# A graph-network and feed-forward kernel: a weight sum moved from GpSimd to VectorE in the opening of the first batch, with the message bias behind it and two distance products some taps later

## Chip, cores and metric

The kernel runs on 1 core of one Trainium2 chip. The metric is the device time of one execution in microseconds. The kernel is written with explicit queues: each engine (TensorE, called PE in the profile; VectorE, DVE; ScalarE, ACT; GpSimd, POOL; SyncE, SP) works through its own list of instructions in order, and semaphores tie the lists together.

## The reference

The input is `x` of 8 batches x 1024 nodes x 128 features and an adjacency `adj` of 8 x 1024 x 1024. A layer norm feeds a graph layer, whose result is added to `x`; a second layer norm feeds a feed-forward layer of the 511 highest-weighted nodes of each batch. What matters here is the graph layer:

```python
xc = jnp.transpose(x, (0, 2, 1))
h = _bn(_conv1d(xc, conv1_w, 0), bn1_g, bn1_b, bn1_m, bn1_v)
h = jax.nn.relu(h)
h = _bn(_conv1d(h, conv2_w, 8), bn2_g, bn2_b, bn2_m, bn2_v)
x_conv = jnp.transpose(jax.nn.relu(h + xc), (0, 2, 1))
s = x @ w_se.T + b_se
sq = jnp.sum(s * s, axis=-1)
dist = sq[:, :, None] + sq[:, None, :] - 2.0 * jnp.einsum('bnd,bmd->bnm', s, s)
A = jnp.exp(-dist) * mask
msg = jax.nn.relu(x @ w_msg.T + b_msg)
x_nmp = jnp.einsum('bnm,bmd->bnd', A, msg)
```

`conv2_w` is 128 x 128 x 17, a convolution of 17 taps along the nodes; `mask` is `adj`. A GRU cell joins `x_conv`, `x_nmp` and `x`.

## The kernel before, in words

**Batches.** A loop over 8 batches runs on every engine; `step(b, ...)` is one batch, and the branches marked `first` are the opening, in which the weights are made ready too. Each batch has: transposition of the normed nodes, the convolution of one tap (`conv1`), the embedding `s`, the messages, the 17-tap convolution, 16 units of distances and adjacency (`adjacency`), and the GRU.

**Two-part numbers.** Products are made in three passes (`three`, L1381 to L1383): weights and data are split into a rounded part ("hi", made by a ScalarE copy) and the rest ("lo", made by a VectorE subtraction). `hi_of_weights(n)` and `lo_of_weights(n)` (L845 and L1016) do so for one piece of the weights, and count `wH_ok` and `wL_ok`.

**The 17-tap convolution** is cut by node parity and tap parity, and each part again, so that sums of taps stand in for some of the taps. PE works through it in five parts: `conv_common` (sums of all), `conv_even_common` (5 taps on `eF`, weights W_PE), `conv_even` (9 taps, weights W_WE), and `conv_odd` (12 taps numbered n = 0 to 11: n = 0 to 3 into bank N1 with weights W_PO, n = 4 to 11 into bank C0 with weights W_WO). Each tap is three matmuls of 128x256. The weights of W_PE and W_PO are sums of two halves of the raw even and odd taps, 128x512 each; `pairs_of_taps(0)` and `pairs_of_taps(1)` (L555) make them on GpSimd into `raw_p`, which lies in the tile `W`. The data of the convolution are differences of phases: `junk` holds `eF` and `fF` (L608, GpSimd), `EF2` (L598 and L599 into `xn`) and `EF3` (L598 and L599 into `tr`) are made on GpSimd, and each is split by ScalarE (L689, L699) and VectorE (L1041 odd row, L1045 pair) into `zR`. `zL_ok` counts these; its sixth step, ZEF3, is the pair of EF3.

**Distances.** `front(b, u)` is a distance product (L1519, one matmul of 128x512 from `U` and `V`) and four transposes of the adjacency (L1525). Three fronts are woven into `conv_odd`, by the table `EARLY`: ahead of taps n = 3, 7 and 11. Front 0 waits for two `distance_operands` on VectorE (L1095, one half of U, one of V), front 1 for the third. From front 3 on, a front is followed by one product with the messages (L1548), three units behind. Each unit on VectorE is one `weigh` (L1127).

**What stands in `conv_odd`'s way.** Ahead of n = 0 it waits for `lo_of_weights(W_PO)` and the odd row of fF; ahead of n = 4 for `common_of_b` (L1051) and for ZEF3:

```python
if row == 1:
    i.then_inc(cc_ps, 1)
    wait(pe, g1_ok, b, 1, 1)
    wait(pe, zL_ok, b, NZ, ZEF3)
for k in range(KQ):
    if n in EARLY:
        front(b, EARLY[n])
```

`add_msg_bias` (L1086) adds the message bias on VectorE, two halves that read PSUM banks D0 and D1; `relu_msg` on ScalarE follows it.

Of the kernel before, what the change touches and what calls it, by code (L numbers as in the profile page):

```python
# [19 lines left out]
ALU = mybir.AluOpType  # L20
# [6 lines left out]
D = 128  # L27
# [12 lines left out]
KQ = KO // 2  # L40
# [17 lines left out]
UV_FOR = {0: 2, 1: 3, NU // 2: 4}  # L58
N2_AT = (5, 6, 7, 8)
EARLY = {3: 0, 7: 1, 11: 2}  # L60


C_ID, C_TRI, C_MASK = 0, P, 2 * P
# [83 lines left out]
def build(nc, x, adj, vectors, weights, conv2_w, const, out):  # L147
    ctx = ExitStack()
    with ctx:
# [6 lines left out]
        def sem(name):  # L156
            return ctx.enter_context(nc.semaphore(name))
# [78 lines left out]
        raw_p = W  # L236
# [35 lines left out]
        stats1, rstd0_ok, rstd_ok, xn_ok = sem("stats1"), sem("rstd0_ok"), sem("rstd_ok"), sem("xn_ok")  # L272
        mom1, mom2, agg = sem("mom1"), sem("mom2"), sem("agg")
        xT_ps, xT_ok, xTH_ok, xTL_ok = sem("xT_ps"), sem("xT_ok"), sem("xTH_ok"), sem("xTL_ok")
        sum_w, pair_w = sem("sum_w"), sem("pair_w")
        c1_ps, ab_ok, z_ok, zH_ok, zL_ok = sem("c1_ps"), sem("ab_ok"), sem("z_ok"), sem("zH_ok"), sem("zL_ok")
        ef1_ok = sem("ef1_ok")
        p1_ps, c1s_ok, g1_ok, gs_ok = sem("p1_ps"), sem("c1s_ok"), sem("g1_ok"), sem("gs_ok")
# [81 lines left out]
        def taps(at, n):  # L360

            return slice(at * D, (at + n) * D)
# [12 lines left out]
        RAW_E, RAW_O = raw_t[:, taps(T_WE - T_S, KO)], raw_t[:, taps(T_WO - T_S, KO)]  # L375
# [110 lines left out]
        def _(pool):  # L486
# [53 lines left out]
            def inv_std2():  # L540
# [8 lines left out]
            nc.gpsimd.memset(blank[:, 0:R_AT], 0.0).then_inc(blank_ok, 1)  # L549
            nc.gpsimd.iota(blank[:, R_AT:R_AT + 1].bitcast(I32), [[1, 1]], base=B * N,  # L550
                           channel_multiplier=0).then_inc(blank_ok, 1)
            def pairs_of_taps(k):

                raw = (RAW_E, RAW_O)[k]
                nc.gpsimd.tensor_tensor(raw_p[:, k * KQ * D:(k + 1) * KQ * D], raw[:, 0:KQ * D], raw[:, KQ * D:],  # L555
                                        ALU.add).then_inc(pair_w, 1)

            def row_numbers(b, q):
# [71 lines left out]
            def step(b, q, first, last):  # L630
                differences(b, 0)
                if first:
                    pool.wait_ge(c2_in, 16)
                    wait(pool, zL_ok, b, NZ, ZEF1)
                    pairs_of_taps(0)
                differences_of_e(b)
                if not first:
                    state_less_candidate(b - 1, 1, 1 - q)
                differences(b, 1)
                if first:  # L640
                    pairs_of_taps(1)
                differences_of_f(b)
                residual(b, q, 0)
                residual(b, q, 1)
                if first:
                    statistics1(1)
                else:
                    statistics2(b - 1)
                    row_numbers(b - 1, 1 - q)
                    products(b - 1, 1 - q)  # L650
                    base_rows(b - 1, 1 - q)
                    if b > 1:
                        rows_by_rank(b - 2, q, 0)
                        rows_by_rank(b - 2, q, 1)
                if b + 2 < B:
                    statistics1(b + 2)
                state_less_candidate(b, 0, q)
# [16 lines left out]
        def _(act):  # L674
# [87 lines left out]
            def normalise2(b, q, ts):  # L762

                if ts[0] == 0:
                    wait(act, rstd2_ok, b, 1, 1)
                    wait(act, x1_ok, b, NH, NH)
                    if b == 0:
                        act.wait_ge(wL_ok, W_PO + 1)
                        act.wait_ge(pair_w, 2)
                    for s_, v in scattered(q, b):  # L770
                        if v > 0:
                            act.wait_ge(s_, v)
                for t in ts:
                    i = nc.scalar.activation(R[:, q, t, 0:D], xall[:, b % NX, t, :], ACT.Identity,
                                             bias=nmr2[:, b, t:t + 1], scale=rstd2[:, b, t:t + 1])
                if ts[-1] == T - 1:
                    i.then_inc(xn2_ok, 1)
# [75 lines left out]
            def step(b, q, first, last):  # L853
                relu_conv1(b)
                hi_of_odd(b, 0, hab[:, 1, :], ab_ok, NH, NH)
                if first:
                    act.wait_ge(sum_w, 2)
                    hi_of_weights(W_SC)
                    hi_of_weights(W_S)
                hi_of_pair(b, 0, EF1, 0)  # L860
                if first:
                    hi_of_odd(b, 1, eF, z_ok, E_AT, N_DIFF)
                    hi_of_weights(W_WO)
                    embed(b, q, 0)
                    common_part(b)
                    act.wait_ge(pair_w, 1)
                    hi_of_weights(W_PE)
                    embed(b, q, 1)
                    hi_of_pair(b, 1, EF2, EF2_AT)
                    embed_hi(b, q)  # L870
                else:
                    candidate(b - 1, 1)
                    embed(b, q, 0)
                    hi_of_odd(b, 1, eF, z_ok, E_AT, N_DIFF)
                    hi_of_pair(b, 1, EF2, EF2_AT)
                    embed(b, q, 1)
                    common_part(b)
                    embed_hi(b, q)
                hi_of_odd(b, 0, fF, z_ok, F_AT, N_DIFF)
                if first:  # L880
                    act.wait_ge(pair_w, 2)
                    hi_of_weights(W_PO)
                distance_hi(b, q, 0)
                hi_of_pair(b, 0, EF3, EF3_AT)
                distance_hi(b, q, 2)
                relu_msg(b)
                exps(b)
                if not last:
                    copy_xT(b + 1, 1 - q)
                hi_of_nmp(b)  # L890
                if first:
                    act.wait_ge(prep_dve, N_PARAM)
                gates(b, 0)
                candidate(b, 0)
                if last:
                    hi_of_sel(0, 0)
                gates(b, 1)

            over_batches(act, step)


# [36 lines left out]
        def _(dve):  # L938
            TS, TT, STT = nc.vector.tensor_scalar, nc.vector.tensor_tensor, nc.vector.scalar_tensor_tensor
# [73 lines left out]
            def lo_of_weights(n):  # L1013
                raw, dst = PIECES[n]
                dve.wait_ge(wH_ok, HI_ORDER.index(n) + 1)
                TT(dst[:, 1], raw, f32(dst[:, 0]), ALU.subtract).then_inc(wL_ok, 1)  # L1016
# [30 lines left out]
            def common_of_b(b):  # L1047

                wait(dve, p1_ps, b, 2, 2)
                wait(dve, c1s_ok, b, 1, 1)  # L1050
                STT(phases(G1), phases(C0[:, :]), col(V_SC2), on_phases(C1S), ALU.mult, ALU.add).then_inc(g1_ok, 1)  # L1051
# [29 lines left out]
            def add_msg_bias(b):  # L1081
                for h in range(NH):
                    wait(dve, m_ps, b, NH, h + 1)
                    if h == 0:
                        wait(dve, nm_ps, b - 1, NU, NU)
                    TT(msgF[:, h * TH:(h + 1) * TH, :], Db[h][:, :].rearrange("p (t d) -> p t d", t=TH),  # L1086
                       bmsg.unsqueeze(1).broadcast_to([P, TH, D]), ALU.add).then_inc(mb_ok, 1)
# [100 lines left out]
            def step(b, q, first, last):  # L1188
# [8 lines left out]
                if first:  # L1197
                    lo_of_weights(W_WE)
                    lo_of_odd(b, 1, eF, ZE)
                    lo_of_weights(W_PE)  # L1200
                    add_msg_bias(b)
                    lo_of_pair(b, 1, EF2, ZEF2)
                    lo_of_weights(W_WO)
                    lo_of_odd(b, 0, fF, ZF)
                    lo_of_weights(W_PO)
                    common_of_b(b)
                else:
                    add_msg_bias(b)
                    lo_of_odd(b, 1, eF, ZE)
                    lo_of_pair(b, 1, EF2, ZEF2)  # L1210
                    blend(b - 1, 1)
                    common_of_b(b)
                    lo_of_odd(b, 0, fF, ZF)
# [162 lines left out]
        def _(pe):  # L1376
# [78 lines left out]
            def conv_odd(b):  # L1455
                if b == 0:
                    pe.wait_ge(wL_ok, W_PO + 1)
                wait(pe, zL_ok, b, NZ, ZF)
                n = 0
                for out_, at, row in ((N1[:, 0:Q], T_WOC, 0), (C0[:, 0:Q], T_WO, 1), (C0[:, Q:2 * Q], T_WO + KQ, 2)):  # L1460
                    if row == 1:
                        i.then_inc(cc_ps, 1)
                        wait(pe, g1_ok, b, 1, 1)
                        wait(pe, zL_ok, b, NZ, ZEF3)
                    for k in range(KQ):
                        if n in EARLY:
                            front(b, EARLY[n])
                        n += 1
                        cols = slice(k, k + Q)
                        i = three(out_, lambda v: wc2[:, v, (at + k) * D:(at + k + 1) * D], zR[:, 0, 0, row, cols],  # L1470
                                  zR[:, 1, 0, row, cols], k == 0, k == KQ - 1)
                i.then_inc(c2_ps, 1)
# [233 lines left out]
```

## Time and profile before

| what | value |
|---|---|
| median of 3 runs | 562.78 us (562.45 to 562.78) |
| the profiled execution | 561.96 us, of which 560.1 us lie between its first and last instruction |
| PE busy | 544.9 us, 97% of the span |
| DVE busy | 475.0 us, 85% |
| ACT busy | 355.2 us, 63% |
| POOL busy | 276.1 us, 49% |

The opening of the first batch, from 10 to 37 us, is where the change lies. Times in the rows are microseconds from the start of the span, unless marked ns. A row of the timeline gives the start, the time taken, the engine, the source line, the operation, output<-inputs, and, in brackets, how long the engine was idle before it and what ended the idling. Consecutive instructions of one engine overlap by some 0.1 us in such rows, so the step from one start to the next is what an instruction costs in a row of them.

### The profile page before, as it was taken

What the parts mean: (1) busy time and instruction counts of PE and PEld (TensorE: products, weight loads), DVE (VectorE), ACT (ScalarE), POOL (GpSimd) and SP (SyncE); (2) the same over time, 40 slices, a digit from 0 to 9 for tenths busy, and PEclk for the clock granted to TensorE, in tenths of its full rate; (3) what the DMA queues carried; (4) which work ended last, traced back from release to release, by engine and by line L of the source; (5) the groups of instructions that cost most, each with busy time, mean ns of one, the idle gap of its engine ahead of it and who ended that gap; (6) DMA issues with size and microseconds to landing.
All of it is one profiled execution on the core that took longest, in us unless ns stands there. A gap on an engine that the chain in (4) does not pass through costs nothing.

```text
span 560.1 us, 9036 instructions
## 1 busy us (share of the span) xinstructions
PE 544.9 (97%) x2964; PEld 414.8 (74%) x2964; DVE 475.0 (85%) x1056; ACT 355.2 (63%) x617; POOL 276.1 (49%) x346
## 2 busy tenths in 40 slices
PE   7899999999999999999999999999999999989996
PEld 4876798678967896689767986798678966755663
DVE  7997388689898989899999989898979987988722
ACT  5867485856586667748674857575856673645552
POOL 3640354325358444834484546654545265437552
PEclk9999999999999999999999999999999999999999
DMA  8703700270008200750057001800171005402102
GB/s 276 280 0 80 297 0 2 71 305 1 2 11 294 109 2 1 208 207 1 1 136 278 1 2 54 323 2 1 46 282 49 1 1 180 160 12 85 38 33 62
DMA packets 33340, 54.53 MB, mean 97 GB/s; under 512 B 2098, under 2 KB 23051, under 8 KB 33166
## 3 DMA queue, kind: packets, MB, share of 16 engines
q1 hardware_dynamic: 29710, 48.42, 24.8%
q0 software_dynamic: 3584, 5.54, 2.9%
q8 instruction: 24, 0.39, 0.3%
q14 instruction: 22, 0.18, 0.1%
HBM read 44.21 MB, written 13.43 MB: 103 GB/s over the span
## 4 chain that ended last, share of the span: by engine, by line
PE 81%; DVE 11%; issue 3%; ACT 3%; POOL 1%; DMA 0%; DVEq 0%; ACTq 0%; POOLq 0%
PE N L1548 19%; PE M L1525 10%; PE C L1381 7%; PE C L1382 6%; PE C L1383 6%; PE D L1519 5%; PE N L1642 4%; PE N L1381 3%; PE N L1382 3%; PE N L1383 3%; ACT hab L681 2%; PE M L1382 2%; PE M L1381 2%; PE M L1383 2%; DVE tr L1036 2%
## 5 line engine op out<-in xcount | busy, mean ns | idle before, releaser
L787 ACT ACTIVATE tr<-D 128x512 f32<-128x512 f32 x128 | 76.4, 597 | 75.6 <-PE D L1519 73.9
L1525 PEld LDWEIGHTS M<-cst,adjb 128*128 128x128 f32 x512 | 63.8, 141 | 35.5 <-issue 20.8
L1519 PE MATMUL D<-V,U 128*128 128x512 f32 x128 | 89.3, 698 | 0.7 <-DVE V L1095 0.7
L1525 PE MATMUL M<-cst,adjb 128*128 128x128 f32 x512 | 76.8, 272 | 0.6 <-DVE ga L1127 0.6
L581 POOL DMA_INDIRECT sel<-R,ridx x56 | 61.1, 1090 | 16.0 <-issue 13.8
L1548 PE MATMUL N<-ga,msgF 128*128 128x512 f32 x128 | 64.2, 593 | 0.0
L1548 PE MATMUL N<-tz,msgF 128*128 128x512 f32 x128 | 64.2, 593 | 0.0
L1381 PE MATMUL C<-zR,wc 128*128 128x256 f32 x208 | 60.6, 291 | 0.1
L1382 PE MATMUL C<-zR,wc 128*128 128x256 f32 x208 | 58.6, 282 | 0.0
L1383 PE MATMUL C<-zR,wc 128*128 128x256 f32 x208 | 58.5, 281 | 0.0
L1157 DVE TENSOR_SCALAR_CACHE_REDUCE junk<-W,R 128x1024 bf16<-128x1024 f32 (+3 forms) x64 | 51.7, 808 | 3.7 <-ACT W L749 3.7
L1127 DVE TENSOR_TENSOR ga<-tr,M 128x512 f32<-128x512 f32 x64 | 43.5, 680 | 9.5 <-ACT tr L787 9.3
L1127 DVE TENSOR_TENSOR tz<-tr,M 128x512 f32<-128x512 f32 x64 | 43.7, 684 | 7.9 <-ACT tr L787 6.1
L528 POOL TENSOR_TENSOR ga<-xT,gn 128x512 f32<-128x512 f32 x16 | 22.8, 1423 | 43.7 <-ACT gn L839 42.8
L1519 PEld LDWEIGHTS D<-V,U 128*128 128x128 f32 x128 | 24.3, 190 | 23.8 <-ACT tr L787 19.1
L1151 DVE TENSOR_SCALAR_CACHE_REDUCE junk<-W,R 128x128 bf16<-128x128 f32 (+6 forms) x56 | 41.4, 739 | 0.0
L627 POOL TENSOR_TENSOR wk<-tz,xT 128x512 f32<-128x512 f32 x8 | 12.5, 1558 | 58.0 <-DVE tz L1058 58.0
L608 POOL TENSOR_TENSOR junk<-hab 128x521 f32<-128x521 f32 x16 | 19.6, 1225 | 40.8 <-ACT hab L681 40.8
L1381 PEld LDWEIGHTS C<-zR,wc 128*128 128x128 f32 x208 | 39.2, 189 | 0.3 <-issue 0.3
L1383 PEld LDWEIGHTS C<-zR,wc 128*128 128x128 f32 x208 | 39.4, 189 | 0.0
L1382 PEld LDWEIGHTS C<-zR,wc 128*128 128x128 f32 x208 | 39.3, 189 | 0.0
L592 POOL DMA_INDIRECT out<-xn,adjb x28 | 28.4, 1015 | 18.7 <-DVE xn L1311 12.3
(245 smaller groups left out, 1523.9 us busy)
## 6 DMA issues: line engine op xcount, KB each, us to landing
adjb<-in_adj SPq DMA_DIRECT2D x8, 4096.0 KB, 14.9
adjb<-sel SPq DMA_DIRECT2D x7, 516.0 KB, 5.3
xall<-in_x SPq DMA_DIRECT2D x7, 512.0 KB, 5.3
out<-R SPq DMA_DIRECT2D x7, 512.0 KB, 3.6
R<-in_conv_w SPq DMA_DIRECT2D x1, 1088.0 KB, 7.1
sel<-R,ridx POOLq DMA_INDIRECT x56, 3.5
xall<-in_weights SPq DMA_DIRECT2D x1, 832.0 KB, 9.8
xall<-in_x SPq DMA_DIRECT2D x2, 256.0 KB, 2.8
```

The lines of the kernel that those rows point to most:

```text
L581: nc.gpsimd.indirect_dma_start(sel[b], bass.IndirectOffsetOnAxis(ap=ridx[:, q, t:t + 1], axis=0), R[:, q, t, :], None, bounds_check=KEEP - ...
L592: nc.gpsimd.indirect_dma_start(out_rows, bass.IndirectOffsetOnAxis(ap=at, axis=0), O[:, p, c, :], None, bounds_check=B * N - 1, oob_is_err ...
L787: nc.scalar.activation(E[:, u % NE, :], Db[u % NH][:, :], ACT.Exp, scale=-1.0).then_inc(exp_ok, 1)
L1127: TT(A[u % NA], E[:, u % NE, :], Mb[u % NH][:, :], ALU.mult).then_inc(A_ok, 1)
L1151: TS(junk[:, t % 2, 0:t * P], W[:, 0:t * P], R[:, q, t, R_W:R_W + 1], None, ALU.is_ge, ALU.add, accum_out=acc[:, 0, t:t + 1])
L1157: TS(junk[:, k, t * P:N], W[:, t * P:], w, None, ALU.is_gt, ALU.add, accum_out=acc[:, 1, t:t + 1])
L1381: MM(out_, wgt(0), hi, start=start, stop=False)
L1382: MM(out_, wgt(0), lo, start=False, stop=False)
L1383: return MM(out_, wgt(1), hi, start=False, stop=stop)
L1519: MM(Db[h][:, :], U[:, t * P:(t + 1) * P], V[:, half(h)], start=True, stop=True).then_inc(d_ps, 1)
L1525: i = TR(Mb[h][:, k * P:(k + 1) * P], adjb[:, h * TH + k, t * P:(t + 1) * P], ident)
L1548: MM(Nb[h][:, :], msgF[:, t, :], A[v % NA], start=t == 0, stop=t == T - 1).then_inc(nm_ps, 1)
```

## The change

Three edits, all of which touch the first batch alone:

1. `pairs_of_taps(1)`, the sum for W_PO, is no longer on GpSimd. VectorE makes it right behind `lo_of_weights(W_PE)`, and a semaphore of its own, `pair_o`, tells ScalarE.
2. `add_msg_bias` moves on VectorE from behind `lo_of_weights(W_PE)` to behind `lo_of_weights(W_PO)`.
3. In the first batch fronts 0 and 1 stand ahead of taps n = 7 and n = 9 and no longer of n = 3 and n = 7; front 2 stays at n = 11.

```diff
+EARLY_0 = {7: 0, 9: 1, 11: 2}
...
                 differences(b, 1)
-                if first:
-                    pairs_of_taps(1)
                 differences_of_f(b)
...
                 if first:
-                    act.wait_ge(pair_w, 2)
+                    act.wait_ge(pair_o, 1)
                     hi_of_weights(W_PO)
...
                     lo_of_weights(W_PE)
-                    add_msg_bias(b)
+                    TT(raw_p[:, KQ * D:], RAW_O[:, 0:KQ * D], RAW_O[:, KQ * D:], ALU.add).then_inc(pair_o, 1)
                     lo_of_pair(b, 1, EF2, ZEF2)
                     lo_of_weights(W_WO)
                     lo_of_odd(b, 0, fF, ZF)
                     lo_of_weights(W_PO)
+                    add_msg_bias(b)
                     common_of_b(b)
...
                     for k in range(KQ):
-                        if n in EARLY:
-                            front(b, EARLY[n])
+                        early = EARLY_0 if b == 0 else EARLY
+                        if n in early:
+                            front(b, early[n])
```

VectorE's list in the opening, from `lo_of_weights(W_PE)` to `common_of_b`, before:

```order
L1016 TENSOR_TENSOR wc<-W,wc 128x512
L1086 TENSOR_TENSOR msgF<-D,vec 128x512 x2
L1045 TENSOR_TENSOR zR<-xn,zR 128x520
L1016 TENSOR_TENSOR wc<-R,wc 128x1024
L1041 TENSOR_TENSOR zR<-junk,zR 128x260
L1016 TENSOR_TENSOR wc<-W,wc 128x512
L1051 SCALAR_TENSOR_TENSOR tz<-C,vec,tr 128x512
```

and of the changed kernel (its line numbers are lower by one up to the new line 1200):

```order
L1015 TENSOR_TENSOR wc<-W,wc 128x512
L1200 TENSOR_TENSOR W<-R 128x512
L1044 TENSOR_TENSOR zR<-xn,zR 128x520
L1015 TENSOR_TENSOR wc<-R,wc 128x1024
L1040 TENSOR_TENSOR zR<-junk,zR 128x260
L1015 TENSOR_TENSOR wc<-W,wc 128x512
L1085 TENSOR_TENSOR msgF<-D,vec 128x512 x2
L1050 SCALAR_TENSOR_TENSOR tz<-C,vec,tr 128x512
```

The pair sum `W<-R` stands where the two halves of the message bias stood, and these are now the last work ahead of `common_of_b`. Behind it both lists go on alike.

GpSimd's list over the same stretch, before:

```order
L555 TENSOR_TENSOR W<-R 128x512
L598 TENSOR_TENSOR xn<-junk 128x260
L599 TENSOR_TENSOR xn<-junk 128x260
L608 TENSOR_TENSOR junk<-hab 128x521
L555 TENSOR_TENSOR W<-R 128x512
L598 TENSOR_TENSOR tr<-junk 128x260
L599 TENSOR_TENSOR tr<-junk 128x260
L627 TENSOR_TENSOR wk<-tz,xT 128x512
```

The second `L555` is gone in the changed kernel, and the rest stands in the same order.

PE's list in `conv_odd`, from the last matmul of tap n = 3 over the taps n = 4, 5 and 6 to front 0 ahead of n = 7, in the changed kernel:

```order
L1383 MATMUL N<-zR,wc 128x256
L1381 MATMUL C<-zR,wc 128x256
L1382 MATMUL C<-zR,wc 128x256
L1383 MATMUL C<-zR,wc 128x256
L1381 MATMUL C<-zR,wc 128x256
L1382 MATMUL C<-zR,wc 128x256
L1383 MATMUL C<-zR,wc 128x256
L1381 MATMUL C<-zR,wc 128x256
L1382 MATMUL C<-zR,wc 128x256
L1383 MATMUL C<-zR,wc 128x256
L1520 MATMUL D<-V,U 128x512
L1526 MATMUL M<-cst,adjb 128x128 x4
```

Before, a `L1519` and its `L1525 x4` stood three matmuls ahead of the first of these C rows, between the taps n = 2 and n = 3. Now nothing but convolution stands ahead of n = 4's wait for EF3.

## Rows read from the trace of the kernel before

**Rows 1.** The page: busy time of each engine, share of the span, instructions

```profile
PE 544.9 (97%) x2964; PEld 414.8 (74%) x2964; DVE 475.0 (85%) x1056; ACT 355.2 (63%) x617; POOL 276.1 (49%) x346
```

**Rows 2.** Waits of PE from 10 to 75 us: total us, times, longest

```profile
PE N L1381 <- DVE wc L1016: 1.3, 2, 0.9
```

**Rows 3.** Timeline of PE in the opening

```profile
23.93 0.36 PE L1381 MATMUL C<-zR,wc 128*128 128x256 f32 x1
...
27.12 0.28 PE L1383 MATMUL C<-zR,wc 128*128 128x256 f32 x1
27.87 0.38 PE L1381 MATMUL N<-zR,wc 128*128 128x256 f32 x1 [0.47 <-DVE wc L1016]
...
29.94 0.47 PE L1519 MATMUL D<-V,U 128*128 128x512 f32 x1 [0.74 <-DVE V L1095]
...
30.60 0.36 PE L1381 MATMUL N<-zR,wc 128*128 128x256 f32 x1
...
31.03 0.28 PE L1381 MATMUL C<-zR,wc 128*128 128x256 f32 x1
...
35.24 0.40 PE L1519 MATMUL D<-V,U 128*128 128x512 f32 x1
```

**Rows 4.** Timeline of DVE in the opening

```profile
12.91 0.69 DVE L1187 TENSOR_TENSOR R<-R 128x512 f32<-128x512 f32 x1
...
20.99 0.69 DVE L1016 TENSOR_TENSOR wc<-W,wc 128x512 fp32r<-128x512 f32 x1 [0.41 <-ACT wc L845]
21.60 1.28 DVE L1086 TENSOR_TENSOR msgF<-D,vec 128x512 f32<-128x512 f32 x2
22.94 0.85 DVE L1045 TENSOR_TENSOR zR<-xn,zR 128x520 fp32r<-128x520 f32 x1
23.71 2.31 DVE L1016 TENSOR_TENSOR wc<-R,wc 128x1024 fp32r<-128x1024 f32 x1
25.94 0.84 DVE L1041 TENSOR_TENSOR zR<-junk,zR 128x260 fp32r<-128x260 f32 x1
26.71 1.10 DVE L1016 TENSOR_TENSOR wc<-W,wc 128x512 fp32r<-128x512 f32 x1
27.74 0.74 DVE L1051 SCALAR_TENSOR_TENSOR tz<-C,vec,tr 128x512 f32<-128x512 f32 x1
...
29.72 0.69 DVE L1045 TENSOR_TENSOR zR<-tr,zR 128x520 fp32r<-128x520 f32 x1
...
36.41 0.67 DVE L1127 TENSOR_TENSOR ga<-tr,M 128x512 f32<-128x512 f32 x1
```

**Rows 5.** Timeline of POOL in the opening

```profile
13.31 1.25 POOL L608 TENSOR_TENSOR junk<-hab 128x521 f32<-128x521 f32 x1 [3.86 <-ACT hab L681]
...
21.02 1.14 POOL L599 TENSOR_TENSOR xn<-junk 128x260 f32<-128x260 f32 x1
22.12 1.11 POOL L608 TENSOR_TENSOR junk<-hab 128x521 f32<-128x521 f32 x1
23.20 1.74 POOL L555 TENSOR_TENSOR W<-R 128x512 f32<-128x512 f32 x1
24.89 1.61 POOL L598 TENSOR_TENSOR tr<-junk 128x260 f32<-128x260 f32 x1
26.46 0.80 POOL L599 TENSOR_TENSOR tr<-junk 128x260 f32<-128x260 f32 x1
```

**Rows 6.** Timeline of ACT: the hi parts of EF2 and of fF

```profile
22.27 0.64 ACT L699 ACTIVATE zR<-xn 128x520 fp32r<-128x520 f32 x1
...
23.85 0.43 ACT L689 ACTIVATE zR<-junk 128x260 fp32r<-128x260 f32 x1
```

**Rows 7.** The chain that ended last, just behind the opening: start, us, what

```profile
37.17 0.61 PE M L1525 x4
```

**Rows 8.** Windows at the span's end: busy time, granted clock, DMA

```profile
557.00:558.00 1.00, 0.00 (x0) 0.00 (x0) 0.27 (x2) 0.00 (x0) 0.00 (x0) 1.00 0.00 0
558.00:559.00 1.00, 0.00 (x0) 0.00 (x0) 0.00 (x0) 0.00 (x0) 0.00 (x0) 1.00 0.75 220
559.00:560.10 1.10, 0.00 (x0) 0.00 (x0) 0.00 (x0) 0.00 (x0) 0.00 (x0) 0.66 0.14 38
```

More of the change, by code:

```diff
@@ L274, in build @@
         xT_ps, xT_ok, xTH_ok, xTL_ok = sem("xT_ps"), sem("xT_ok"), sem("xTH_ok"), sem("xTL_ok")
-        sum_w, pair_w = sem("sum_w"), sem("pair_w")
+        sum_w, pair_w, pair_o = sem("sum_w"), sem("pair_w"), sem("pair_o")
         c1_ps, ab_ok, z_ok, zH_ok, zL_ok = sem("c1_ps"), sem("ab_ok"), sem("z_ok"), sem("zH_ok"), sem("zL_ok")
@@ L551, in _, with pairs_of_even_taps @@
                            channel_multiplier=0).then_inc(blank_ok, 1)
-            def pairs_of_taps(k):
-                raw = (RAW_E, RAW_O)[k]
-                nc.gpsimd.tensor_tensor(raw_p[:, k * KQ * D:(k + 1) * KQ * D], raw[:, 0:KQ * D], raw[:, KQ * D:],
+            def pairs_of_even_taps():
+                nc.gpsimd.tensor_tensor(raw_p[:, 0:KQ * D], RAW_E[:, 0:KQ * D], RAW_E[:, KQ * D:],
                                         ALU.add).then_inc(pair_w, 1)
@@ L634, in step @@
                     wait(pool, zL_ok, b, NZ, ZEF1)
-                    pairs_of_taps(0)
+                    pairs_of_even_taps()
                 differences_of_e(b)
@@ L768, in normalise2 @@
                         act.wait_ge(wL_ok, W_PO + 1)
-                        act.wait_ge(pair_w, 2)
+                        act.wait_ge(pair_w, 1)
+                        act.wait_ge(pair_o, 1)
                     for s_, v in scattered(q, b):
@@ L880, in step @@
                 if first:
-                    act.wait_ge(pair_w, 2)
+                    act.wait_ge(pair_o, 1)
                     hi_of_weights(W_PO)
```

## The prediction

> **What bounds the kernel now.** I read the page first: PE is busy for 97% of the span [rows 1], so a microsecond counts only where PE loses it, and what PE loses early is lost at the end, unless a later wait takes it up. Next I asked for PE's waits from 10 to 75 us. In the stretch of the change, from 21 us on, they are two: 0.47 us ahead of `conv_odd`'s first tap, for `lo_of_weights(W_PO)`, and 0.74 us ahead of front 0, for the second distance operand [rows 2, 3]. (The 1.3 us of rows 2 hold the first of these and one wait near 16 us, ahead of all that is changed.) Behind front 0 the list of waits names no other, so nothing up to 75 us can take up a delay. The third view was the timeline of DVE and POOL side by side. The reader is to see there that DVE works without a pause from 20.99 us to the distances, so that it sets when W_PO, the operands and EF3 are ready, and that some of its rows are long for their size [rows 4].
>
> Those rows are the key. A subtraction of 128x512 takes 0.69 us at 20.99 and 1.10 us at 26.71; one of 128x260 takes 0.84 us at 25.94, longer than the 0.69 us of one twice its size. Each long row began while a POOL operation was under way, and ended a fixed time behind it [rows 4, 5]:
> - POOL L555 ends at 24.94, the DVE 128x1024 at 26.02: 1.10 us after it, about its bare time.
> - POOL L598 ends at 26.50, the DVE 128x260 at 26.78: 0.28 after it.
> - POOL L599 ends at 27.26, the DVE 128x512 at 27.81: 0.55 after it. For the 128x520, 23.23 to 23.79: 0.56.
>
> It holds the other way too. POOL's 128x260 takes 0.80 us by itself and 1.61 at 24.89; it ends 0.48 us behind the DVE operation that ends at 26.02, as the one at 26.46 ends 0.48 behind 26.78, and that at 21.02 ends 0.48 behind 21.68. L608 ends 0.96 behind the DVE end at 13.60 [rows 4, 5]. So an operation of DVE with both inputs in SBUF and one of POOL exclude each other and take turns. The message bias, which reads PSUM, takes 1.28 us for two beside a POOL operation: it does not take part.
>
> The Trainium skill (SBUF — State Buffer, "Who interferes with whom") states this as an exclusive hold for the whole instruction, between a VectorE instruction with two SBUF inputs and a GpSimd one that reads SBUF; the rows agree. It speaks against a hope in this change, that a POOL operation was free for DVE or is free now.
>
> **The change part by part.** I walk both lists from 20.99 us, where nothing has changed yet, with the turn-taking above. Ends in brackets are those of before.
> - `lo_of_weights(W_PE)` ends at 21.68 (21.68). POOL L599, which waits for it, ends at 22.16 (22.16).
> - New pair sum on DVE. No row shows it on this engine. It has the size of the 128x512 subtractions: 0.69 us bare, 0.55 behind a release, 1.10 if blocked [rows 4]; 0.55 to 1.10 bounds it. It comes at 21.60, is blocked until 22.16, and ends at 22.71. I take that.
> - POOL L608 (fF) was free here; now it ends 0.96 behind, at 23.67 (23.23).
> - EF2's pair on DVE: its hi part is there at 22.91 [rows 6], so it is behind L608: 23.67 + 0.56 = 24.23 (23.79).
> - POOL L598 comes next, as L555 with its 1.74 us is gone: 24.71. DVE 128x1024: + 1.10 = 25.81 (26.02). POOL L599: 26.29 (27.26). DVE odd row of fF: + 0.29 = 26.58 (26.78); its hi part, 0.43 us behind L608 [rows 6], is long done.
> - `lo_of_weights(W_PO)` starts at 26.50 with POOL idle: 0.69, so 27.19 (27.81). Its hi part needs the pair sum of 22.71, and ScalarE comes to it behind fF, near 24.3: no wait.
> - Message bias: two PSUM reads, start at 27.11, and the next instruction can start 1.22 us later, at 28.33. `common_of_b` started at 27.74 [rows 4].
>
> So DVE gives back 0.6 us of blocking and takes on 1.22 us: from `common_of_b` on, everything is 0.59 us later. EF3's pair started at 29.72 and ended at 30.41 [rows 4]; now it ends at 31.00. The moved bias itself costs nothing further: ScalarE's relu of the messages came behind its distance operands, near 29.3, and the bias ends at 28.4.
>
> PE now. `conv_even` waits for EF2's pair and started at 23.93, 0.14 behind it; now 24.37. Its 27 matmuls took 23.93 to 27.24, 3.31 us or 0.368 a tap [rows 3], so it ends at 27.68. W_PO is there (27.19), so the wait of 0.47 is gone: `conv_odd` starts at 27.7 (27.87), a gain of 0.2. Four taps take it to 29.15. There it stops, at n = 4, for EF3 until 31.1: a wait of 2 us in place of the 0.74. Before, front 0 and tap n = 3 stood across this moment, and EF3 (30.41) was ready when PE came to n = 4 at 31.03 [rows 3, 4]. The later place of fronts 0 and 1 takes away the one piece of work that could lie ahead of EF3. Had front 0 stayed at n = 3, its operands would be ready 0.59 later too, at 30.4, ahead of EF3.
>
> From n = 4 to front 3, eight taps and fronts 1 and 2 took 31.03 to 35.24, 4.21 us. Now front 0 is in the stretch as well, 0.66 us (29.94 to 30.60), and a tap behind a wait costs 0.1 more (0.38 against 0.28 in its first row) [rows 3]. So front 3 starts at 31.1 + 4.21 + 0.66 + 0.1 = 36.07, against 35.24: 0.83 later. A little comes back at once. The transposes of front 4 took 0.61 in the chain where the others take 0.44 [rows 7], since they waited 0.17 us for the third `weigh`, which ended at 37.08 [rows 4]; that is now 0.59 later, at 37.67, and PE comes there at 37.83, so the wait is gone: 0.83 - 0.17 = **0.66 us later**. Moving fronts 0 and 1 to 7 and 9 keeps their exponentials ahead of front 2, and `weigh` 0 at 33.8 and 1 at 34.8 ahead of fronts 2 and 3: no new wait.
>
> The sum is made in the profiled execution: 561.96 + 0.66 = 562.6 us. That execution is 0.82 below the median of the runs; against the median 562.78 the forecast is 563.4 us. What a measurement of this kernel can tell from no change is about 0.2%, or 1.1 us; so I forecast no measurable difference, on the slow side.
>
> **The rivals.**
> - *The lock gives nothing back (slower).* If POOL's phase differences take the port at worse moments, for instance just ahead of `lo_of_weights(W_PO)` so that it again takes 1.10 us and ends at 27.8, the full 1.22 of the bias plus the 0.14 for PE's restart falls on EF3 and PE: front 3 about 1.45 late, 1.3 at the end, 564.1. It decides the sign from 1.13 us on, that is when W_PO ends later than about 27.65. For it: before, the DVE operation was blocked at just this place. Against it: one POOL operation of four is gone. A milder form, in which DVE wins the first turn at 21.60, gives W_PO at 27.49, 0.3 later than forecast, and the end near 563.7. Chance 17%.
> - *No blocking of the new order (faster, too little to measure).* If DVE were never blocked, EF2's pair would end at 23.6, 0.15 earlier, with 24.8 for the 128x1024 and about 25.7 for W_PO; PE's `conv_even` would end near 27.1 and EF3's pair near 29.5, so PE waits 1 us and front 3 starts at 34.45, 0.8 early: 562.0. Against it stand all the long rows. Chance 12%.
> - *The clock falls in the new 2 us wait.* Then the stretch behind it, 4.97 us long, runs at 1.2 instead of 2.4 GHz and costs up to 5 us more: 568. Against it: at the span's end PE does nothing from 557 to 559, and the granted clock is still 1.00 in both windows, and falls only in the next [rows 8]. Chance 3%.
>
> The Trainium skill (TensorE: Matmul & The Clock Gate, "Part 1") makes the slow clock the default that activity lifts, and that a long idle stretch brings back; by that rule a wait of 2 us is a step toward it. The rows at the end show 2 us at least without it.
>
> That the change does nothing at all is excluded: the lists of all three engines differ as described.
>
> **How the numbers follow.** The forecast has 68%, with 562.9 to 563.9 as its own range (the 0.55 to 1.10 of the pair sum, either winner of the turns, 0.3 us of spread between runs). To leave out no more than 2 in 10 the range takes in the slower rival and leaves out the fast one and the clock: 562.3 to 564.4. Faster by over 0.2% (under 561.65) needs more than the fast rival: 0.04. Slower by over 0.2% (over 563.91): most of the slower rival, the clock, a tail of the forecast: 0.20. Same: 0.76.
>
> **What would show it.** In the changed profile: PE idle 0 ahead of `conv_odd`'s first tap, and about 2 us ahead of the first C tap, ended by DVE's zR from `tr`; the pair sum on DVE 1.1 us long, started at 21.6; W_PO's subtraction 0.69 long, ended near 27.2; `common_of_b` at 28.3; front 3 at 36.1; transposes of front 4 at 37.8. The prediction is wrong if the wait ahead of n = 4 is under 1.2 us, if the DVE rows stay long where POOL is idle, or if PE finds another wait behind 37 us in which 0.66 us vanish.

## The result and the profile after

| | before | changed |
|---|---|---|
| median, 20 runs each | 562.78 us (562.15 to 563.5) | 563.34 us (562.7 to 565.03) |
| ratio | | 1.0013, 95% interval 1.0007 to 1.0019 |
| profiled execution | 561.96 us, span 560.1 | 564.65 us, span 562.6 |

The changed kernel is 0.13% slower, 0.4 to 1.1 us: a loss too small for the 0.2% of a single comparison, and visible with 20 runs on each side. The forecast was 563.4. But its executions spread over 2.3 us where those of before spread over 1.4, and the profiled one is the second slowest of the 20, so its trace has to be read in two parts.

The first part is the opening itself. The rows of DVE in the changed kernel, by the timeline:

```profile
21.48 0.69 DVE L1015 TENSOR_TENSOR wc<-W,wc 128x512 fp32r<-128x512 f32 x1 [0.41 <-ACT wc L844]
22.09 1.10 DVE L1200 TENSOR_TENSOR W<-R 128x512 f32<-128x512 f32 x1
23.42 1.30 DVE L1044 TENSOR_TENSOR zR<-xn,zR 128x520 fp32r<-128x520 f32 x1 [0.23 <-ACT zR L697]
24.64 1.64 DVE L1015 TENSOR_TENSOR wc<-R,wc 128x1024 fp32r<-128x1024 f32 x1
26.20 0.84 DVE L1040 TENSOR_TENSOR zR<-junk,zR 128x260 fp32r<-128x260 f32 x1
26.97 0.68 DVE L1015 TENSOR_TENSOR wc<-W,wc 128x512 fp32r<-128x512 f32 x1
27.57 1.27 DVE L1085 TENSOR_TENSOR msgF<-D,vec 128x512 f32<-128x512 f32 x2
28.77 0.73 DVE L1050 SCALAR_TENSOR_TENSOR tz<-C,vec,tr 128x512 f32<-128x512 f32 x1
...
30.75 0.69 DVE L1044 TENSOR_TENSOR zR<-tr,zR 128x520 fp32r<-128x520 f32 x1
```

and those of POOL beside them:

```profile
22.61 1.55 POOL L608 TENSOR_TENSOR junk<-hab 128x521 f32<-128x521 f32 x1
24.24 0.96 POOL L598 TENSOR_TENSOR tr<-junk 128x260 f32<-128x260 f32 x1
25.16 1.60 POOL L599 TENSOR_TENSOR tr<-junk 128x260 f32<-128x260 f32 x1
```

In this execution W_PE's subtraction starts at 21.48 where it started at 20.99 [rows 4], so all that comes before the change was 0.49 us late, and 0.49 is to be taken off every time of this trace. Then the reader sees the walk of the prediction: the pair sum blocked to 1.10 us and ended at 22.70 (forecast 22.71), EF2's pair at 24.23 (24.23), W_PO at 27.16 (27.19), `common_of_b` started at 28.28 (28.33), EF3 ended at 30.95 (31.00). W_PO's subtraction is 0.68 us long, with POOL idle, where it was 1.10 [rows 4].

The rows of PE in the changed kernel:

```profile
24.86 0.36 PE L1381 MATMUL C<-zR,wc 128*128 128x256 f32 x1 [0.58 <-DVE zR L1044]
...
28.15 0.28 PE L1381 MATMUL N<-zR,wc 128*128 128x256 f32 x1
...
31.58 0.36 PE L1381 MATMUL C<-zR,wc 128*128 128x256 f32 x1 [1.84 <-DVE zR L1044]
...
38.12 0.39 PE L1520 MATMUL D<-V,U 128*128 128x512 f32 x1
```

The wait ahead of `conv_odd`'s first tap is gone and 1.84 us stand ahead of n = 4, ended by EF3's pair, as forecast. The last row is front 3. Less 0.49, it starts at 37.63, and the forecast was 36.07: 1.56 us too many.

The second part is where these went. Windows of the changed kernel: length, busy time of PE, PE's weight loads, DVE, ACT and POOL, granted clock, DMA share, GB/s:

```profile
28.00:32.00 4.00, 2.16 (x18) 1.99 (x17) 4.00 (x7) 1.89 (x4) 0.00 (x0) 1.00 0.00 0
32.00:36.00 4.00, 4.00 (x22) 3.65 (x21) 2.77 (x5) 0.75 (x2) 2.43 (x2) 0.61 0.00 0
36.00:40.00 4.00, 4.00 (x28) 3.28 (x27) 3.37 (x11) 1.64 (x3) 1.53 (x6) 0.97 0.00 0
```

and the chain that ended last, in that stretch (start, length, what):

```profile
32.77 0.12 PE C L1383
32.89 0.36 PE D L1520
33.25 0.85 PE M L1526 x4
34.11 0.21 PE C L1381
...
35.39 0.43 PE D L1520
35.81 0.72 PE M L1526 x4
36.53 0.12 PE C L1381
```

The granted clock is 0.61 in the mean from 32 to 36 us: TensorE went from 2.4 to 1.2 GHz, and not in the wait but 1.3 us after its end. Through the wait itself the clock reads 1.00 (28 to 32 us). The matmul of a tap takes 0.21 us in place of 0.12, a distance product 0.36 to 0.43 in place of 0.24, and four transposes 0.72 to 0.85 in place of 0.44. From 32.89 to 36.53 these pieces add up to 3.64 us; at the durations around them they would be 2.08. The difference, 1.56, is the whole of the surplus.

Of the 20 executions of the changed kernel 4 show a mean clock of 0.996 and spans of 562.2 to 562.6 us, while the other 16 have 0.997 or more and 560.9 to 561.9. The span is the time from the first to the last instruction. By this the fall comes in some executions only and costs 1.45 us by the medians of the spans, and the median of all 20 hardly holds it. Not every high time is a fall: two executions of 564.12 and 564.18 us have spans of 561.2 and 561.3, so what they lost lies outside the span.

### The profile page after: what moved, and what is told of

It is laid out like the page before. It is cut to its first block, busy times and chain, and to the rows that moved or that the text cites. A ratio compares the mean times of both kernels' runs of the same rounds, so it can differ in the third digit from the quotient of the medians.

```text
span 562.6 us, 9036 instructions
## 1 busy us (share of the span) xinstructions
PE 545.6 (97%) x2964; PEld 415.9 (74%) x2964; DVE 475.6 (85%) x1057; ACT 355.0 (63%) x617; POOL 274.5 (49%) x345
## 4 chain that ended last, share of the span: by engine, by line
PE 82%; DVE 9%; ACT 3%; issue 3%; POOL 1%; DMA 1%; DVEq 0%; ACTq 0%; POOLq 0%
PE N L1549 20%; PE M L1526 10%; PE C L1381 7%; PE C L1382 6%; PE C L1383 6%; PE D L1520 5%; PE N L1643 4%; PE N L1381 3%; PE N L1382 3%; PE N L1383 3%; ACT hab L679 2%; PE M L1382 2%; PE M L1381 2%; PE M L1383 2%; DVE tr L1035 2%
```

## The experiments

Every ratio is against runs of the kernel before on the same chip, with its 95% interval. To compare profiles, whose openings start up to half a microsecond apart, I also give times from the start of the first sum of the raw taps (DVE, `R<-R 128x1024`, 11.66 us in before). On that scale front 3 starts at 23.58 us in before, W_PO ends at 16.15, and the second batch's transposes start at 44.51.

### e1. Edit 3 alone: the fronts late

```diff
+EARLY_0 = {7: 0, 9: 1, 11: 2}
...
-                        if n in EARLY:
-                            front(b, EARLY[n])
+                        early = EARLY_0 if b == 0 else EARLY
+                        if n in early:
+                            front(b, early[n])
```

> Edit 3 alone: fronts 0 and 1 late, the pair sum and the message bias as before. Turn-taking theory: VectorE and GpSimd keep every start of before, EF3's pair ends at 30.4, PE comes to tap n = 4 near 29.4 and waits 1.1 to 1.2 us there; front 3 starts 0.28 us later than before (in a profile whose VectorE list runs at the same times), and 0.17 comes back at front 4: +0.1 us, ratio 1.0002. Clock theory (a wait of PE of about 2 us lets TensorE's clock fall in part of the executions): this wait is the shorter one, granted clock 1.00 and no execution over 563.9. Rival (the late fronts themselves cost, by exponentials and weigh steps that come late): +0.5 us or more with the clock at 1.00.

Measured: 562.91 us, ratio 0.9997 (0.9988 to 1.0006), highest execution 563.43. PE's rows:

```profile
30.75 0.36 PE L1382 MATMUL C<-zR,wc 128*128 128x256 f32 x1 [0.98 <-DVE zR L1046]
...
35.69 0.40 PE L1521 MATMUL D<-V,U 128*128 128x512 f32 x1
```

The wait stands at n = 4, 0.98 us (forecast 1.1 to 1.2), and front 3 starts at 23.82, 0.24 later (forecast 0.28). The second batch's transposes start at 44.58, 0.07 later. Edit 3 costs nothing that can be measured, and its rival is out.

### e2. The change without edit 3

```diff
-                        early = EARLY_0 if b == 0 else EARLY
-                        if n in early:
-                            front(b, early[n])
+                        if n in EARLY:
+                            front(b, EARLY[n])
```

> The change without edit 3: pair sum on VectorE, bias late, fronts at n = 3, 7 and 11. Turn-taking theory: VectorE's list is that of the changed kernel, front 0 waits for the second operand until about 0.6 us later than before, and the third weigh, 0.59 late, sets front 4: +0.6 us, ratio 1.0010. Clock theory: PE's wait is about 1.5 us in place of 1.84, the clock may still fall in some executions; if it does not, the highest execution stays below 564.3. Rival (edit 3 is what costs): back to 562.8.

Measured: 563.6 us, ratio 1.0010 (1.0001 to 1.0019), highest 563.8; PE waits 1.60 us ahead of front 0, and no execution shows the clock below 0.998. So the loss belongs to edits 1 and 2, and the late fronts neither caused it nor gave anything back that could be measured. With front 0 at n = 3 the wait is 0.24 us shorter, and no execution shows a fallen clock. That the shorter wait is the reason is not shown: if 4 in 20 executions fell here as well, 11 in a row without a fall would still come about one time in twelve, and e4 shows falls with front 0 at n = 3.

### e3. Edit 1 alone: the pair sum on VectorE

GpSimd's second sum goes, VectorE makes it, the bias comes directly behind it, and the fronts are those of before.

```diff
                     lo_of_weights(W_PE)
+                    TT(raw_p[:, KQ * D:], RAW_O[:, 0:KQ * D], RAW_O[:, KQ * D:], ALU.add).then_inc(pair_o, 1)
                     add_msg_bias(b)
```

> Edit 1 alone: the pair sum on VectorE, the message bias directly behind it (it was directly behind W_PE), fronts as before. Turn-taking theory: W_PO's subtraction ends near 27.5 in place of 27.8, common_of_b and all behind it start 0.3 us earlier, PE waits as before for operands, front 3 0.3 us earlier: -0.3 us, ratio 0.9995. Rival (an added VectorE operation costs its 0.6 us, since VectorE is the engine that PE waits for): +0.6 us, ratio 1.001.

Measured: 562.82 us, ratio 0.9994 (0.9985 to 1.0003). DVE's rows:

```profile
22.01 1.10 DVE L1200 TENSOR_TENSOR W<-R 128x512 f32<-128x512 f32 x1
...
24.24 1.10 DVE L1044 TENSOR_TENSOR zR<-xn,zR 128x520 fp32r<-128x520 f32 x1
25.26 1.64 DVE L1015 TENSOR_TENSOR wc<-R,wc 128x1024 fp32r<-128x1024 f32 x1
26.82 0.41 DVE L1040 TENSOR_TENSOR zR<-junk,zR 128x260 fp32r<-128x260 f32 x1
27.16 0.68 DVE L1015 TENSOR_TENSOR wc<-W,wc 128x512 fp32r<-128x512 f32 x1
```

VectorE got one operation more, blocked to 1.10 us, and `common_of_b` starts 0.38 us earlier (15.70 against 16.08), as do front 3 (23.21, 0.37 earlier) and the second batch (44.13). PE's wait is not where it was forecast. It stands ahead of `conv_even`, for EF2's pair, which is 1.15 us later behind the pair sum and the bias, and PE no longer stops for W_PO and only 0.1 us for front 0:

```profile
25.48 0.36 PE L1381 MATMUL C<-zR,wc 128*128 128x256 f32 x1 [1.27 <-DVE zR L1044]
```

The rival, that an operation added to the engine that is waited for costs its length, would have been +0.6. Taking an operation off GpSimd gave VectorE more than the operation cost it. The interval of the times holds 1; the trace shows the sign.

### e4. Edit 2 alone: the bias late

```diff
-                    add_msg_bias(b)
                     lo_of_pair(b, 1, EF2, ZEF2)
...
                     lo_of_weights(W_PO)
+                    add_msg_bias(b)
```

> Edit 2 alone: the message bias behind W_PO, the pair sum on GpSimd, fronts as before. Turn-taking theory: VectorE stands idle 1.2 us ahead of EF2's pair, nothing is blocked less, all from common_of_b on is 1.22 us later, and so is front 0: +1.2 us with the clock up, ratio 1.0022. Clock theory: PE waits about 2.1 us for the second operand, as long as in the changed kernel or longer; the clock falls in at least a part of the executions and adds about 1.5 us to those: spread to 565.5. Rival (the bias is hidden wherever it stands): within 0.3 us of before.

Measured: 564.24 us, ratio 1.0026 (1.0017 to 1.0035). Three of 11 executions show a clock of 0.995 and spans of 563.3 to 563.6, the other eight spans of 562.0 to 562.6. The bias late costs 1.2 us by itself (median span 562.3 against 561.1 of before on this chip), and the clock sometimes another 1.3. Both theories hold so far. The pause of DVE in this kernel:

```profile
21.63 1.00 DVE L1016 TENSOR_TENSOR wc<-W,wc 128x512 fp32r<-128x512 f32 x1 [1.86 <-ACT wc L845]
23.57 1.84 DVE L1045 TENSOR_TENSOR zR<-xn,zR 128x520 fp32r<-128x520 f32 x1 [0.94 <-ACT zR L699]
```

It stands idle for 0.94 us where the bias was, and makes the bias up at the end. `common_of_b` starts 1.44 us later than before, 0.2 more than forecast, and the first row shows where 0.2 can come from: W_PE's subtraction ended 0.68 later than in before (see e9). PE waits 1.56 us ahead of front 0 in this trace, and the clock stays up. The three executions that fell have no trace. If W_PE was on time in them, the wait was near 2.0 us (an estimate: the 0.74 of before and the bias's 1.22), so it is not known to be 1.56.

### e5. PE's wait filled

```diff
                     if row == 1:
+                        if b == 0:
+                            for _ in range(14):
+                                i = MM(N1[:, Q:2 * Q], wc2[:, 0, T_WOC * D:(T_WOC + 1) * D], zR[:, 0, 0, 0, 0:Q],
+                                       start=True, stop=True)
                         i.then_inc(cc_ps, 1)
```

> The changed kernel with 14 extra matmuls of 128x256 on PE between tap n = 3 and the wait ahead of n = 4, into a part of bank N1 that nobody reads: 14 x 0.118 = 1.65 us of work in a wait of 1.84. Nothing is left out. Turn-taking theory alone: the wait shrinks to 0.2 us, PE goes on at the same time, the time is that of the changed kernel with all its spread. Clock theory: the clock stays at 1.00 from 24 to 44 us, no execution over 563.9, median 563.2 to 563.4. Rival (the executions above 564 of the changed kernel have another cause): the highest executions stay at 564.5 to 565.

Measured: 563.63 us (563.33 to 563.82), ratio 1.0012 (1.0003 to 1.0021), span 561.5 to 561.9 in all 11. From 28 to 32 us, and from 32 to 36, in the columns of the windows above:

```profile
28.00:32.00 4.00, 4.00 (x36) 4.00 (x35) 4.00 (x7) 2.01 (x4) 0.00 (x0) 1.00 0.00 0
32.00:36.00 4.00, 4.00 (x34) 3.76 (x33) 3.51 (x6) 1.20 (x2) 2.21 (x2) 1.00 0.00 0
```

The high executions are gone, and what stays by the times is 0.66 us (563.63 against 562.97), the size of the forecast. In the trace W_PE's subtraction ended late (10.70), and the second batch starts at 45.39, 0.88 later than before. With that lateness PE's wait ahead of n = 4 would have been about 1.4 us without the filling (an estimate: against e0 below, PE is 0.68 later and EF3 0.27), and the 14 matmuls cover it with 0.2 to spare.

### e0. The changed kernel again, on the same chip

> The changed kernel once more, beside the filled one on the same chip: ratio 1.0010 to 1.0016, between a tenth and four tenths of its executions 0.8 us or more above the rest. Clock theory: a profile of it shows the clock at 1.00 or fallen for some 3 us behind 32 us, as the execution falls.

Measured: 564.98 us (563.43 to 565.37), ratio 1.0032 (1.0020 to 1.0043). Four of seven executions have a clock of 0.995 or 0.996 and spans of 563.2 to 563.3; the other three have 0.998 or more and 561.6 to 562.2. More than the one to four tenths that I expected fell. The profile is of one that did not:

```profile
28.00:32.00 4.00, 2.16 (x19) 1.99 (x18) 4.00 (x8) 1.74 (x3) 0.00 (x0) 1.00 0.00 0
32.00:36.00 4.00, 4.00 (x35) 3.77 (x33) 3.50 (x7) 1.41 (x3) 2.58 (x2) 1.00 0.00 0
```

and its wait ahead of n = 4:

```profile
31.43 0.36 PE L1381 MATMUL C<-zR,wc 128*128 128x256 f32 x1 [1.84 <-DVE zR L1044]
```

Its wait is 1.84 us as well and PE is busy for 2.16 us between 28 and 32, but 35 matmul records stand from 32 to 36 us, not 22. On the common scale every row of VectorE from W_PE to EF3 and the end of PE's wait agree with the trace that fell, to 0.02 us. Front 3 starts at 24.37, 0.79 later than before (forecast 0.83), and the second batch 0.61 later (forecast 0.66). Beside the filled kernel, on the same chip, this shows the cause of the large spread: with the stretch 4 of 7 executions fell, with the stretch filled 0 of 11. The three with the clock up have a median of 563.66 us, 0.69 above before; the four others lie 1.4 above these (spans 563.25 against 561.9), and between the two traces the second batch differs by 1.6 (46.73 and 45.12).

### e6. EF3's pair ahead of the operands

```diff
+                if first:
+                    lo_of_pair(b, 0, EF3, ZEF3)
                 distance_operands(b, q, (0, 1))
-                lo_of_pair(b, 0, EF3, ZEF3)
+                if not first:
+                    lo_of_pair(b, 0, EF3, ZEF3)
```

> The changed kernel with EF3's subtraction ahead of the first two distance operands on VectorE. Turn-taking theory: EF3 ends 1.3 us earlier, the wait ahead of n = 4 falls from 1.84 to about 0.6 us, front 3 starts 1.2 us earlier than in the changed kernel; but the third weigh, which comes behind moments1 on VectorE, is as late as before and sets front 4: the end is only 0.1 us earlier than the changed kernel's, +0.55 us against before, ratio 1.0010. Clock theory: clock at 1.00, no high executions. Rival (PE's wait ahead of n = 4 is the whole loss): -0.4 us against before.

Measured: 563.5 us, ratio 1.0010 (1.0001 to 1.0019), clock 0.997 or more in all 11. The transposes of front 4:

```profile
38.26 0.66 PE L1529 MATMUL M<-cst,adjb 128*128 128x128 f32 x4 [0.39 <-DVE ga L1126]
```

The time came out as forecast, the way there only in part. EF3 and tap n = 4 come 1.1 us earlier than in the changed kernel, but front 3 starts at 23.89, 0.5 earlier and not 1.2, since PE now stops 0.2 us ahead of front 0 for its operand and 0.3 ahead of front 2's transposes for the first weigh. And the half microsecond does not reach the end: the third weigh ends at 26.16 us where it ended at 25.42 before (25.95 in e0), and PE waits for it; the second batch starts at 45.26, 0.14 later than in e0. The late bias has a second way to the end, past every wait of `conv_odd`.

### e7. The same, and the moments late

The edit of e6, and with it:

```diff
-                    if u == 1:
-                        if first:
-                            moments1(1)
-                        else:
-                            moments2(b - 1)
+                    if u == 3 and first:
+                        moments1(1)
+                    if u == 1 and not first:
+                        moments2(b - 1)
```

> As e6, and the moments of batch 1 on VectorE two weigh steps later (behind the fourth, not the second). If the third weigh is what holds e6 up, front 4 is free 1.3 us earlier on VectorE's side, and the end is set by PE: 0.3 to 0.5 us below before, ratio 0.9992 to 0.9996. Rival (the later moments hold up the fifth weigh and with it front 6, or the weigh steps from u = 4 on): as e6, 1.0010.

Measured: 563.0 us, ratio 1.0002 (0.9993 to 1.0012). The third weigh ends at 24.64 and sets nothing; the moments late are worth 0.5 us here by the times and 0.58 at the second batch (44.68 against 45.26), so the weigh was the holder. But the forecast of 0.3 to 0.5 us below before was missed: front 3 starts at 23.90, 0.3 later than before and not earlier. Front 0 waits for its operands, W_PO was 0.25 us later than in the changed kernel by the early turn (see e9), and front 2's transposes wait 0.3 us for the first weigh.

### e8. The moments late in the kernel before

The edit to the moments shown for e7, alone, on the kernel before.

> The kernel before, with the moments of batch 1 two weigh steps later on VectorE and nothing else. In before the transposes of front 4 wait 0.17 us for the third weigh; this frees it: -0.15 to -0.2 us, ratio 0.9997. If the later moments hold up the fifth weigh: no change or +0.2.

Measured: 562.7 us, ratio 0.9996 (0.9987 to 1.0005); the second batch starts at 44.35, 0.16 earlier, which is the 0.17 us that I had read off [rows 7]. It cannot be told from no change by the times.

### e9. The bias woven in

The pair sum on VectorE, the fronts of before:

```diff
+                    add_msg_bias(b, (0,))
                     lo_of_pair(b, 1, EF2, ZEF2)
+                    add_msg_bias(b, (1,))
                     lo_of_weights(W_WO)
...
                     lo_of_weights(W_PO)
-                    add_msg_bias(b)
                     common_of_b(b)
```

> The pair sum on VectorE, the two halves of the message bias (which read PSUM) put where VectorE would otherwise be blocked by GpSimd: the first behind the pair sum, the second behind EF2's pair; fronts as before. Turn-taking theory: the bias then costs VectorE next to nothing, common_of_b starts 0.5 us earlier than before and 1.1 earlier than in the changed kernel, EF2 comes as early as in the changed kernel, PE waits about 0.6 us for front 0, front 3 is 0.5 us earlier than before: -0.5 us, ratio 0.9991. Rival (VectorE's own busy time decides, and the order within it does not): as the pair sum alone, ratio 0.9994 at best.

Measured: 563.04 us (562.22 to 564.35), ratio 0.9998 (0.9989 to 1.0007). That is short of the -0.5 us, and it does not rule out the rival, by which the order within VectorE's list gives nothing beyond the pair sum. The profiled execution (563.07) shows the bias unblocked at 0.68 us a half, but `common_of_b` at 16.42, 0.34 later than before, and all behind it late by as much. The lateness comes in earlier in the list:

```profile
19.32 0.41 DVE L1040 TENSOR_TENSOR zR<-junk,zR 128x260 fp32r<-128x260 f32 x1
21.58 1.00 DVE L1015 TENSOR_TENSOR wc<-W,wc 128x512 fp32r<-128x512 f32 x1 [1.85 <-ACT wc L844]
```

with, on POOL:

```profile
18.40 2.49 POOL L555 TENSOR_TENSOR W<-R 128x512 f32<-128x512 f32 x1 [3.59 <-DVE zR L1044]
```

and the same two operations in before:

```profile
19.07 1.51 DVE L1041 TENSOR_TENSOR zR<-junk,zR 128x260 fp32r<-128x260 f32 x1
18.15 2.14 POOL L555 TENSOR_TENSOR W<-R 128x512 f32<-128x512 f32 x1 [3.59 <-DVE zR L1045]
```

In before the 128x260 of eF's odd row took 1.51 us, blocked behind the first pair sum. Here it takes 0.41 and the pair sum waits for it, 2.49 us long, and W_PE ends 0.66 later (10.68 against 10.02). I call this the early turn, and the order of before the good one. The new pair sum, 1.60 us long here and 1.10 in the changed kernel, then ends 1.16 later.

### e10. The bias woven in, and the moments late

> As e9, and the moments of batch 1 two weigh steps later. The third weigh no longer sets front 4, 0.17 us more come back: -0.7 us, ratio 0.9988. If the moments cost as much later, as e9.

Measured: 562.81 us, ratio 0.9991 (0.9982 to 1.0001). The spans of its 11 executions are 560.1, 560.4, 560.5, 560.5 and then 561.0 to 561.4, against 560.9 to 561.4 of before. Four executions lie 0.6 to 1.0 us below the median of before, 561.1, and seven between 0.1 below and 0.3 above it. The profiled one is of the upper seven (561.4): its 128x260 went first as in e9, and its second batch starts at 44.66, 0.15 later than before.

### e11. The early turn fixed

```diff
                     lo_of_weights(W_WE)
+                    dve.wait_ge(pair_w, 1)
                     lo_of_odd(b, 1, eF, ZE)
```

> As e10, with one wait added on VectorE: the 128x260 subtraction of eF's odd row waits until GpSimd's first pair sum is done. In the profiles of e4, e5, e6, e7, e9 and e10 that subtraction took the port ahead of the pair sum, which made W_PE 0.67 us later; in those of before, the changed kernel, e0, e1 and e3 it came behind. Theory (the two groups of e10's executions, spans 560.1 to 560.5 and 561.0 to 561.4 us, are the two orders of this turn): with the order fixed all executions fall in the lower group, -0.7 us against before, ratio 0.9988, W_PE's subtraction ends 10.0 us behind the start of the first sum. Rival (the groups have another cause): two groups as in e10, and ratio 0.9991 to 0.9993.

Measured: 562.06 us (562.0 to 562.18) against 562.55, ratio 0.9990 (0.9981 to 0.9999). All 11 spans are 560.2 or 560.3, where the same chip's runs of before are 560.4 to 560.9. DVE's rows:

```profile
20.70 0.83 DVE L1040 TENSOR_TENSOR zR<-junk,zR 128x260 fp32r<-128x260 f32 x1 [1.19 <-POOL W L555]
21.46 1.10 DVE L1015 TENSOR_TENSOR wc<-W,wc 128x512 fp32r<-128x512 f32 x1
```

There is one group, as expected, and the span varies by 0.1 us. The rest of the forecast missed. W_PE ends at 10.53 and not at 10.0: the odd row no longer starts with the pair sum but behind it, runs into POOL L598, and W_PE's subtraction into L599. `common_of_b` starts at 16.26 and front 3 at 23.76, each 0.18 later than before, and with the 0.17 us of the late moments the second batch starts at 44.51, exactly as in before. So the 0.5 us of the times (562.06 against 562.55, with an interval that only just leaves out 1) is not found in the opening of the trace, and where it comes from stays open.

That the two groups of e10 are the two orders of the turn is not shown either. The upper group was seen in a profile, the lower was not; e10 ran on another chip, where the spans of before vary from 560.9 to 561.4, and was not repeated beside e11. And in e3, whose profiled execution of 560.8 us has the good order, two executions of 560.3 stand apart from nine of 560.8 to 561.3: half a microsecond can differ for another reason. This version has the lowest ratio of all, 0.9990, which cannot be told from the 0.9991 of e10.

## Why the prediction was right, point by point

- **What bounds the stretch.** Right. PE waits for VectorE's list, and each wait of the changed kernel in this stretch is ended by the DVE operation named. One sentence was too wide: that nothing up to 75 us could take up a delay. The list of waits does not show the 0.17 us at front 4 that the same prediction then uses, and e6 and e8 show that the third weigh does hold PE there.
- **The turn-taking.** Right, to 0.05 us at each of five points of VectorE's list, and right again for the edits apart: pair sum alone -0.38 in the trace (forecast -0.3), bias late alone +1.2 us by the spans of the executions with the clock up (forecast +1.2), both together +0.54 at `common_of_b` in e0 (forecast +0.59). Apart they add up to +0.8, in the forecasts to +0.9: what an operation costs here depends on what stands beside it. The order of the first turn, the odd row of eF against the first pair sum, was taken to stay, since the lists are unchanged up to there. It stayed in both traces of the changed kernel, but not in those of six other kernels whose lists are just as unchanged up to there; that it stayed is luck.
- **The pair sum at 1.10 us.** Right; it was the value for a blocked operation, and it is blocked.
- **The bias at 1.22 us.** Right: the edit that costs. Before, it lay under GpSimd's operations and ScalarE's copy of EF2; at the new place VectorE does nothing else with that time.
- **Front 3 0.83 later, 0.17 given back.** Right: 0.79 in a profile with the clock up, and 0.61 at the next batch. The time of front 4's transposes was added up wrongly: 37.17 and 0.83 are 38.00 and not 37.83. They start at 37.95 on the scale of before, without a wait, and the conclusion stands.
- **The clock.** This is the term that was mis-sized. I gave the fall 3% and up to 5 us, as if the clock stayed down to front 3. By the mean clocks it fell in 4 of 20 and 4 of 7 executions. It cost 1.56 us in the trace and 1.4 by the medians, since it was back after 3.6. The step that failed is the argument from the span's end, where the clock still stood at 1.00 after 2 us without work [rows 8]. It stood at 1.00 all through the wait of the changed kernel too, and fell 1.3 us behind it, as it fell at the span's end in the next row. So a clock of 1.00 during an idle stretch did not tell what it would be when the work went on. The rule of the Trainium skill (TensorE: Matmul & The Clock Gate, "Part 1"), that the slow clock comes back after an idle stretch, pointed this way. The page speaks of a longer stretch than the 1.84 us that were enough here, so the measurement decides on the size.
- **The number.** 563.4 against 563.34, and 562.3 to 564.4 holds it. Part of that is luck: in the runs of e0, on another chip, where more than half of the executions fell, the median was 564.98, outside the range, against 562.97 of before, and a forecast without the clock would have missed there.

## What to carry to other kernels

Where VectorE and GpSimd block each other, price an edit by both lists walked together, turn by turn: an operation moved from GpSimd to VectorE gained 0.38 us here, and an operation that reads PSUM, moved out of GpSimd's shadow, lost 1.2. The idle stretch of 1.84 us on TensorE had a second price here, the clock, paid in some executions only: look at the spread of the runs and not at the median alone. A trace of one execution holds one order of the turns: before the next edit is priced, see whether the order of before still stands. And when a gain stops at a wait, look for the next engine whose list carries the same delay, as the third weigh did.

## What was not expected of the hardware

- **The clock falls on a short wait.** In the trace it fell 1.3 us after PE had resumed from a wait of 1.84 us (31.58 to 32.89), stayed at 1.2 GHz for 3.6 us of continuous work, and came back. By the mean clocks this happened in 4 of 20 and 4 of 7 executions of the changed kernel and in 3 of 11 of e4, whose profiled execution waited 1.56 us and kept the clock; in none of 11 of e2, whose profile shows 1.60 us, nor in any with 0.98 us (e1) or with the stretch filled (e5). The two traces of the changed kernel agree to 0.02 us up to the end of the wait, and one fell and one did not: what picks the execution stays open.
- **The turn can change with an edit elsewhere.** With the same instructions ahead of it, the 128x260 of VectorE went before GpSimd's waiting pair sum in the profiles of e4, e5, e6, e7, e9 and e10 (0.41 us long, pair sum 2.49) and behind it in those of before, the changed kernel and e0 to e3 and e8 (1.51 and 2.14). W_PE then ends at 10.7 or 10.0 us, except in e2, whose scale starts 0.3 earlier. Both traces of the changed kernel have the same order; whether the order also changes between executions of one kernel was not seen.
